# Token tiles 4 to 15 of the projections: normalised rows pass through DRAM and are turned by 32x32 blocks on VectorE

## What is computed

```
x  = L0_attn_x                                  # (2, 1024, 1024) float32
xn = (x - mean(x)) / sqrt(var(x) + 1e-5)        # over the last axis
q, k, v = xn @ wq, xn @ wk, xn @ wv             # 1024 -> 32, 8, 8 heads of 32
q, k = rope(q), rope(k)                         # pairs of neighbours rotated
s = softmax(q @ k.T / sqrt(32) + causal) @ v    # four query heads to one key head
s = s @ wo
w_gu, w_d = 4-bit weights times scales
h = silu(xn @ w_gu[:, :2752]) * (xn @ w_gu[:, 2752:])
out = x + s * silu(h @ w_d)
```

## Time and profile before

| | |
|---|---|
| median of 3 runs | 2204.02 us |
| time of the profiled execution | 2204.33 us |
| its span, first to last instruction | 2202.6 us |
| TensorE busy | 99% of the span |
| VectorE, GpSimd, ScalarE busy | 69%, 61%, 46% |
| granted TensorE clock, mean | 0.999 |

### The profile page before, as it was taken

One profiled execution on the slowest core, in us unless ns is written; L12 is line 12 of the kernel. 1 busy time (PEld: TensorE's weight loads), 2 busy tenths in 40 slices (PEclk: granted clock), 3 DMA queues, 4 the chain that ended last, 5 costly groups with the idle time before them and its releaser, 6 DMA issues.

```text
span 2202.6 us, 39253 instructions
## 1 busy us (share of the span) xinstructions
PE 2179.7 (99%) x14856; PEld 1106.4 (50%) x14856; DVE 1523.5 (69%) x2272; ACT 1014.1 (46%) x1918; POOL 1334.6 (61%) x1398
## 2 busy tenths in 40 slices
PE   7999999999999999999999999999999999999998
PEld 4555545555555555555555555444444444444443
DVE  5677767777777777777777773377858865555564
ACT  4333156666666666666666667344322221111211
POOL 4855588788878887888878888367620013332332
PEclk9999999999999999999999999999999999999999
DMA  6344212433243332333333333455359874333332
GB/s 206 99 109 101 48 33 59 74 64 59 63 76 76 68 51 71 71 73 69 59 66 66 74 52 61 72 164 172 101 163 327 277 262 149 110 110 110 110 116 89
DMA packets 296128, 230.01 MB, mean 104 GB/s; under 512 B 191664, under 2 KB 260782, under 8 KB 292868
## 3 DMA queue, kind: packets, MB, share of 16 engines
q1 hardware_dynamic: 295940, 227.51, 39.9%
HBM read 136.54 MB, written 90.78 MB: 103 GB/s over the span
## 4 chain that ended last, share of the span: by engine, by line
PE 97%; DVE 1%; ACT 1%; issue 1%; POOL 0%; DMA 0%; DVEq 0%; ACTq 0%; POOLq 0%
PE gu_ps L1183 39%; PE out_ps L1897 9%; PE qk_ps L726 9%; PE out_ps L1877 8%; PE mx_ps L1080 6%; PE sc_ps L1124 6%; PE dn_ps L1886 5%; PE dn_ps L1897 4%; PE o_ps L1146 4%; PE v_ps L709 2%; PE o_ps L1150 2%; PE sz_ps L1093 2%; PE sz_ps L1098 1%; PE tr_ps L695 1%; PE dn_ps L1889 1%
## 5 line engine op out<-in xcount | busy, mean ns | idle before, releaser
L1183 PE MATMUL gu_ps<-xT,wg 128*128 128x512 f16 x4128 | 983.7, 378 | 0.4 <-DVE h L1454 0.4
L1518 POOL TENSOR_TENSOR room<-room 128x1152 f16<-128x1152 f32 x256 | 539.2, 2106 | 40.7 <-ACT room L1232 27.8
L1183 PEld LDWEIGHTS gu_ps<-xT,wg 128*128 128x128 f16 x4128 | 367.7, 97 | 377.6 <-DVE h L1454 0.9
L1232 ACT ACTIVATE room<-sc_ps 128x512 f32<-128x512 f32 (+3 forms) x768 | 349.0, 489 | 369.1 <-PE sc_ps L1124 365.4
L2244 POOL TENSOR_TENSOR xT<-arena,xT 128x1024 f16<-128x1024 f32 x40 | 85.1, 2129 | 411.1 <-ACT xT L2012 411.1
L1513 POOL TENSOR_SCALAR_AFFINE_SELECT room<-room 128x128 f32<-128x128 f32 x512 | 143.8, 296 | 140.8 <-ACT room L1232 140.8
L1361 DVE TENSOR_REDUCE part<-mx_ps 128x2 f16<-128x1024 f32 x128 | 157.0, 1227 | 100.3 <-PE mx_ps L1080 100.2
L1361 DVE TENSOR_REDUCE shift<-mx_ps 128x2 f16<-128x1024 f32 (+3 forms) x256 | 212.8, 831 | 8.8
L726 PE MATMUL qk_ps<-xT,w 128*128 128x512 f16 x960 | 212.8, 379 | 0.0
L1124 PE MATMUL sc_ps<-arena 97*128 97x512 f16 (+3 forms) x768 | 209.7, 327 | 2.3 <-ACT room L1232 2.1
L1146 PE MATMUL o_ps<-arena,room 128*128 128x65 f16 x2240 | 191.1, 191 | 0.0
(11 more groups left out here) (181 smaller groups left out, 3203.1 us busy)
## 6 DMA issues: line engine op xcount, KB each, us to landing
hidden_scratch<-hT SPq DMA_DIRECT2D x84, 256.0 KB, 3.0
o_scratch<-room SPq DMA_DIRECT2D x64, 260.0 KB, 9.7
room<-o_scratch SPq DMA_DIRECT2D x16, 1040.0 KB, 7.7
hT_in<-hidden_scratch SPq DMA_DIRECT2D x11, 1344.0 KB, 7.5
arena<-q_scratch SPq DMA_DIRECT2D x48, 256.0 KB, 3.8
stock<-in_qw_d SPq DMA_DIRECT2D x42, 256.0 KB
down_scratch<-wd SPq DMA_DIRECT2D x84, 128.0 KB, 2.8
xin<-in_x SPq DMA_DIRECT2D x16, 512.0 KB, 4.6
```

Source lines behind the costliest of these rows:

```text
L1183: last = pe.matmul(to[:, :], wg[:, u, wp, s, cols], xT[:, xp, s, tokens], start=(s == 0 and k == 0), stop=(s == KT - 1 and k == 2))
L1232: act.activation(probs[:, r % 2, START[t] + c:START[t] + e], sc_ps[n % SC_BANKS][:, 0:e - c], ACT.Exp, scale=float(1.0 / np.sqrt(HD))).the ...
L1518: pool.tensor_tensor(p_lo[:, r % 2, c], probs[:, r % 2, c], p_hi[:, r % 2, c], ALU.subtract).then_inc(lo_done, 1)
```

## The change

Tiles 0 to 3 are handled as before. For tiles 4 to 15 the halves are no longer formed and turned on TensorE. The float32 rows `xn` are stored to a DRAM scratch tensor and loaded back by four transfers, each to 32 partitions, so that 32 tokens lie on 32 partitions four times over. VectorE turns the 32x32 blocks with four instructions into one float32 tile `x32`; ScalarE copies `x32` to the high half of `xT`, and GpSimd subtracts that from `x32` into the low half. The schedule tables are new, `SPLIT_AT` and `LOAD_AT` are added. `x32` is also the buffer into which x tile 2 is loaded. `xh` and `xl` share their memory with the two buffers `xt`. In the later stages a wait of VectorE for its own reciprocal goes, and two semaphores become one.

```diff
-        xin = sb("xin", [P, XB, D], F32)
+        two_in = sb("xin", [P, 2, D], F32)
         xn = sb("xn", [P, 2, D], F32)
-        xh = sb("xh", [P, 2, D], F16)
-        xl = sb("xl", [P, 2, D], F16)
+        xt = sb("xt", [P, 2, D], F32)
+        x32 = sb("x32", [P, D], F32)
+        xin = [two_in[:, 0, :], two_in[:, 1, :], x32[:, :]]
...
-        NORM_AT = {0: 0, 2: 1, 4: 2, 5: 3}
-        TURN_AT = {3: 0, 5: 1, 7: 2, 8: 3}
+        NORM_AT = {0: 0, 1: 1, 3: 2, 5: 3}
+        LOAD_AT = {1: 0, 2: 1, 4: 2, 6: 3}
+        TURN_AT = {3: 0, 5: 1, 6: 2, 8: 3}
+        SPLIT_AT = {4: 0, 6: 1, 7: 2, 9: 3}
...
             def load_x(n):
-                if n >= XB:
-                    sp.wait_ge(xn_done, n - XB + 1)
+                if n >= 3:
+                    sp.wait_ge(xn_done, {3: 2, 4: 1}.get(n, n - 1))
...
+            def store_normed(n):
+                sp.wait_ge(xn_done, n + 1)
+                sp.dma_start(xn_d[n], xn[:, n % 2, :]).then_inc(xn_stored[n % 2], 16)
+
+            def load_turned(n):
+                if n < CHT + 2:
+                    sp.wait_ge(xh_turned, CHT)
+                    sp.wait_ge(xl_turned, CHT)
+                else:
+                    sp.wait_ge(xt_turned, n - CHT - 1)
+                sp.wait_ge(xn_stored[n % 2], 16 * ((n - CHT) // 2 + 1))
+                for k in range(P // 32):
+                    sp.dma_start(xt[32 * k:32 * (k + 1), n % 2, :].rearrange("j (t c) -> j t c", c=D // 4),
+                                 xn_d[n, :, k * (D // 4):(k + 1) * (D // 4)].rearrange("(t j) c -> j t c", j=32)
+                                 ).then_inc(xt_loaded[n % 2], 16)
...
-            load_x(6)
             for e in range(NCH * CT):
                 tc, j = e // CT, e % CT
+                if tc + 1 < NCH and j in NORM_AT:
+                    store_normed((tc + 1) * CHT + NORM_AT[j])
+                if tc + 1 < NCH and j in LOAD_AT:
+                    load_turned((tc + 1) * CHT + LOAD_AT[j])
                 load_tables(e)
...
# gpsimd, at the end of a step
+            def low_turned(n):
+                tokens = slice(n * P, (n + 1) * P)
+                pool.wait_ge(xTh_done, n + 1)
+                pool.wait_ge(xTl_done, n)
+                pool.tensor_tensor(xT[:, 1, :, tokens], x32[:, :].rearrange("p (s t) -> p s t", s=KT),
+                                   xT[:, 0, :, tokens], ALU.subtract).then_inc(xTl_done, 1)
...
-                if j in NORM_AT and tc + 1 < NCH:
-                    low_x((tc + 1) * CHT + NORM_AT[j])
+                if j in SPLIT_AT and tc + 1 < NCH:
+                    low_turned((tc + 1) * CHT + SPLIT_AT[j])
...
# scalar
+            def high_turned(n):
+                act.wait_ge(xt_turned, n - CHT + 1)
+                act.activation(xT[:, 0, :, n * P:(n + 1) * P], x32[:, :].rearrange("p (s t) -> p s t", s=KT), ACT.Copy
+                               ).then_inc(xTh_done, 1)
...
-                if tc + 1 < NCH and j in TURN_AT:
-                    turned((tc + 1) * CHT + TURN_AT[j])
+                if tc + 1 < NCH and j in SPLIT_AT:
+                    high_turned((tc + 1) * CHT + SPLIT_AT[j])
...
                     spread((tc + 1) * CHT + NORM_AT[j])
-                    high_x((tc + 1) * CHT + NORM_AT[j])
...
# vector
+            def turn(n):
+                dve.wait_ge(xt_loaded[n % 2], 64 * ((n - CHT) // 2 + 1))
+                if n == CHT:
+                    dve.wait_ge(xn_done, 3)
+                else:
+                    dve.wait_ge(xTh_done, n)
+                    dve.wait_ge(xTl_done, n)
+                for k in range(P // 32):
+                    cols = slice(k * (D // 4), (k + 1) * (D // 4))
+                    last = dve.transpose(x32[:, :].rearrange("p (s t) -> p s t", s=KT)[:, :, 32 * k:32 * (k + 1)],
+                                         xt[:, n % 2, cols].rearrange("p (i s) -> p s i", s=KT))
+                last.then_inc(xt_turned, 1)
...
                 tables_at(e)
+                if tc + 1 < NCH and j in TURN_AT:
+                    turn((tc + 1) * CHT + TURN_AT[j])
                 if tc + 1 < NCH and j in NORM_AT:
                     norm((tc + 1) * CHT + NORM_AT[j])
...
# tensor
                 queries_keys(e)
-                if j in TURN_AT and tc + 1 < NCH:
-                    turn((tc + 1) * CHT + TURN_AT[j])
...
# third stage, vector
-            dve.reciprocal(rsum[:, u, :], parts(u)[:, :, HD]).then_inc(rsum_done, 1)
+            dve.reciprocal(rsum[:, u, :], parts(u)[:, :, HD])
...
-            dve.wait_ge(rsum_done, n + 1)
```

More of the change, by code:

```diff
@@ L179, in project_qkv @@
                 g_idx_d, qwg, zw, scw, szt, rest, mid, qwd, idx, gu_loaded, dn_loaded, idx_loaded, table_step,
-                qw_loaded, z_d):
+                qw_loaded, z_d, xn_d):
     bn, mv, std, rstd, eps = small
@@ L210, in project_qkv @@
         sb("fill", [P, room_words - (KT * QKV + 2 * S + 6 * BANK + KV * VW)], F32)
-        xin = sb("xin", [P, XB, D], F32)
+        two_in = sb("xin", [P, 2, D], F32)
         xn = sb("xn", [P, 2, D], F32)
-        xh = sb("xh", [P, 2, D], F16)
-        xl = sb("xl", [P, 2, D], F16)
+        xt = sb("xt", [P, 2, D], F32)
+        x32 = sb("x32", [P, D], F32)
+        xin = [two_in[:, 0, :], two_in[:, 1, :], x32[:, :]]
+        xh = xt[:, 0, :].bitcast(F16).rearrange("p (u c) -> p u c", u=2)
+        xl = xt[:, 1, :].bitcast(F16).rearrange("p (u c) -> p u c", u=2)
         qk_ps = [bank(f"qk_ps{i}", [P, BANK], F32) for i in range(2)]
@@ L241, in project_qkv @@
         xTl_done = sem("xTl_done")
+        xn_stored = [sem(f"xn_stored{i}") for i in range(2)]
+        xt_loaded = [sem(f"xt_loaded{i}") for i in range(2)]
+        xt_turned = sem("xt_turned")
         qk_ready = sem("qk_ready")
@@ L285, in project_qkv, with x_place, x_count @@
         x_v = x.rearrange("b (t p) d -> (b t) p d", p=P)
-        NORM_AT = {0: 0, 2: 1, 4: 2, 5: 3}
-        TURN_AT = {3: 0, 5: 1, 7: 2, 8: 3}
+        NORM_AT = {0: 0, 1: 1, 3: 2, 5: 3}
+        LOAD_AT = {1: 0, 2: 1, 4: 2, 6: 3}
+        TURN_AT = {3: 0, 5: 1, 6: 2, 8: 3}
+        SPLIT_AT = {4: 0, 6: 1, 7: 2, 9: 3}
+        def x_place(n):
+            return 2 if n == 2 else n % 2
+        def x_count(n):
+            return 16 * (n // 2 if n >= 4 and n % 2 == 0 else (n + 1) // 2 if n % 2 else 1)
         def block_of(j):
@@ L313, in load_x @@
             def load_x(n):
-                if n >= XB:
-                    sp.wait_ge(xn_done, n - XB + 1)
-                sp.dma_start(xin[:, n % XB, :], x_v[n]).then_inc(x_loaded[n % XB], 16)
+                if n >= 3:
+                    sp.wait_ge(xn_done, {3: 2, 4: 1}.get(n, n - 1))
+                sp.dma_start(xin[x_place(n)], x_v[n]).then_inc(x_loaded[x_place(n)], 16)
+            def store_normed(n):
[12 more added lines that the diff above has]
+                                 ).then_inc(xt_loaded[n % 2], 16)
             def load_w(i):
@@ L388, in sync @@
                 if j % 2 == 1 and j // 2 < CHT:
-                    n = tc * CHT + j // 2 + 3 + CHT
+                    n = tc * CHT + j // 2 + 2 + CHT
                     if n < TT:
@@ L544, in norm @@
                 u = n % 2
-                dve.wait_ge(x_loaded[n % XB], 16 * (n // XB + 1))
+                own = xin[x_place(n)]
+                dve.wait_ge(x_loaded[x_place(n)], x_count(n))
                 for h in range(2):
-                    last = dve.bn_stats(bn[:, h, :], xin[:, n % XB, h * BANK:(h + 1) * BANK])
+                    last = dve.bn_stats(bn[:, h, :], own[:, h * BANK:(h + 1) * BANK])
                 last.then_inc(bn_done, 1)
@@ L553, in norm @@
                 dve.wait_ge(rstd_done, n + 1)
-                if n >= 2:
+                if 2 <= n < CHT + 2:
                     dve.wait_ge(xl_done, n - 1)
-                dve.tensor_scalar(xn[:, u, :], xin[:, n % XB, :], mv[:, u, 0:1], rstd[:, u, :],
+                if n >= CHT + 2:
+                    dve.wait_ge(xn_stored[u], 16 * ((n - CHT) // 2))
+                dve.tensor_scalar(xn[:, u, :], own, mv[:, u, 0:1], rstd[:, u, :],
                                   ALU.subtract, ALU.mult).then_inc(xn_done, 1)
+            def turn(n):
[10 more added lines that the diff above has]
+                last.then_inc(xt_turned, 1)
             def low_w(i):
@@ L668, in vector @@
                 if e == (NCH - 1) * CT:
-                    dve.wait_ge(xh_done, TT)
-                    dve.wait_ge(xl_done, TT)
+                    dve.wait_ge(xTh_done, TT)
+                    dve.wait_ge(xTl_done, TT)
                 if tc == NCH - 1:
@@ L1617, in finish @@
         FREED = {B_M6: [(0, 1)], B_M7: [(1, 1)], B_M4: [(1, 0), (0, 0)]}
-        rsum_done = sem("rsum_done")
         joined = sem("joined")
@@ L1637, in finish @@
         wk_loaded = sem("wk_loaded")
-        tail_loaded = sem("tail_loaded")
         block_loaded = [sem(f"block_loaded{i}") for i in range(SUMS + 2)]
@@ L1829, in sync @@
```

(8 more changed lines are left out.)

## The result

The changed kernel takes 2241.11 us (median, 2240.53 to 2242.05) against 2204.01 us for the one before; the ratio is 1.0169, with a 95% interval of 1.0151 to 1.0186. It is 37.1 us slower, where I forecast 16 slower and a range up to 2236. The direction was right, the size was not.

What follows compares the result with a forecast made beforehand. TensorE, busy 99% of the time, was taken to bound the kernel. The terms -11.8 + 12.4 + 6.4 + 4.2 + 4.6 = +15.8 us on 2204.3 gave 2220 us, with a range from 2207 to 2236.

Steps and rivals of the forecast that it cites:

- the 11.8 us: TensorE's transpositions of 12 tiles at 0.98 us, all on the path, forecast as won by removing them.
- The direct chain: Each chunk's end: last query and key result through VectorE, ScalarE, GpSimd to the fourth split; wait at least 4.2 us.
- The clock: Slower TensorE clock after gaps: 2.3 us for each of the two longer, nothing for the third, 4.6 us.
- 12.4, 6.4 and 4.2 us: Forecast waits of TensorE at the ends of chunks 0, 1 and 2.
- 1.3 us a tile, which I take: VectorE's four transpositions of a tile, at 0.31 us each from the pace of the 32-lane swap.
- the upper bound of 2.6: VectorE's transpositions of a tile at the pace of the table comparison, 2.6 us for 1024 columns.
- in all 21.6: Chunk 1: us from VectorE's start of step 16 through the three last splits, chained by transpositions.
- so 2.9 us late: Chunk 1: VectorE's lateness from step 15; TensorE's step 16 result leads the values' end by 18.1 us.
- tables of 0.7 us there; it is on time: Chunk 2: short table work, so no late start, and the direct chain's 4.2 us decides.
- Chunk 0: VectorE and GpSimd followed step by step: TensorE waits from 87.1 to 99.5, 12.4 us.
- Slow transpositions: Rival: 2.6 us a tile, 1.3 more, eight in series, 10.4 us more, 2230; chance 18%.
- The late queue: Rival: reloads late, a queue held up by new waits puts each chunk's end some 4 us later, 2232; 8%.

Runs made afterwards that it cites:

- e2: The changed kernel with GpSimd's low half of a turned tile at the start of its step, not the end: 2225.86 us, ratio 1.01.
- e6: The changed kernel with SyncE's load of x and store of the values both ahead of the step's table loads: 2237.62 us, ratio 1.0153.
- e9: As e8, with SyncE's queue reordered (x loads first, table transfers in step 17, heads' loads in steps 25 and 27): 2198.47 us, ratio 0.9978.
- e3: The changed kernel with only SyncE's load of x moved ahead of the step's table loads: 2240.02 us, ratio 1.0165.
- e4: The changed kernel with one of a tile's four transpositions, three quarters of the turned data left out: 2230.72 us, ratio 1.0119.
- e10: As e7, with the same order of SyncE's queue as e9: 2206.96 us, ratio 1.0012.
- e8: As e7, but tiles 4 to 7 turned on TensorE with the old schedule, only tiles 8 to 15 through DRAM: 2209.81 us, ratio 1.0027.
- e7: The changed kernel with the orders of e2 and e6, transpositions ahead of table parts, and a schedule one to two steps earlier: 2218.17 us, ratio 1.0061.

## Why the prediction was right and wrong

**Right:** what bounds the kernel; the 11.8 us; that they would be eaten by a wait of TensorE for GpSimd's low half of the fourth tile at three chunk ends; that the reload lands in time (3.1 and 4.1 us, and no transposition waits for it). The direct chain has the length that I gave it, 6.6 us from the last swap to the end of the split (176.01 to 182.57; 154.89 to 161.5 in the prediction), but it decided no gap: VectorE began it 13.5 us after TensorE's result of 162.46. The clock was put at 4.6 us, 2.3 for each of two gaps and nothing for the third, and measured at 4.4, as 1.4, 1.7 and 1.3. That the sums agree is luck: in e2 to e6 the same three pieces lost 5.9 to 6.7 us.

**Wrong, the sizes of the gaps:** 12.4, 6.4 and 4.2 us were forecast, 23.0 in sum; 14.46, 17.47 and 11.78 came, 43.7. The 20.7 us between them are the whole error. The steps that failed:

1. *VectorE's transpositions, "1.3 us a tile, which I take".* They last 606 ns and follow each other at 0.53 us, 2.13 us a tile. The pace of the swap was the wrong neighbour; the upper bound of 2.6 was nearer. The Trainium skill (VectorE: DVE Perf Modes, "The three transpose paths") has 311 ns for half the elements and a quarter of the bytes per partition; 606 ns agrees with its double, while the tile's 2.13 us goes by the shorter distance of 0.53. The same page's "Rules for kernel authors" names TensorE for a 128x128 transposition whose result may go to PSUM; the whole change, 37.1 us slower, agrees, and e9, in which VectorE turns eight tiles and 5.6 us are won, does not. The term is 0.8 us a tile, so 1.7 us in the chain of chunk 1 and as much in that of chunk 2.
2. *The chain of chunk 1, "in all 21.6".* It was 27.5, in chunk 2 too. Two transpositions account for 1.7 of the 5.9 us between them. 2.9 more are VectorE's own work in step 18: the fourth tile's transposition could have begun when the third split ended, at 168.86 + 2.12 = 170.98, but began at 173.90, behind the sum and a table part (3.0 in chunk 2). I had walked the chain from split to transposition as if VectorE had nothing between. The rest, 1.3, is 0.4 in each of the two ways from swap to split, 6.6 and not 6.2, and 0.5 in the first link.
3. *The start of chunk 1's chain, "so 2.9 us late".* It was 155.12 - 146.9 = 8.2 us late. I looked at SyncE's queue for what the change adds and not for what already stood in it, 9.7 us of table transfers ahead of a load of x that the change issues one tile later. e3 and e6 show both waits that come of it. In e6, without them, it is 3.0 us late. That meets my 2.9 through two errors that cancel: the table part took 1.49 + 1.52 us and not 2.35 + 1.64, and the transposition took 2.2 and not 1.3.
4. *Chunk 2, "tables of 0.7 us there; it is on time".* The 0.7 us are the table part of another step. That of step 25, which corresponds to step 15, was 3.4 us long in the kernel before (its rows stand below this list). In the changed kernel it takes 2.4 us, the transposition follows and then `norm`, and VectorE reaches step 26 at 230.94, when TensorE's result has been there since 223.35 + 5.18 = 228.5: 2.4 us late. So the long chain decides there and not the direct one of 4.2.
5. *Chunk 0* was followed step by step and came within 2.1 us. Two and a half transpositions at 0.8 us are enough for that, and e4 took 4.0 us from this gap, two and a half at 1.6; that it is these alone is worked out, not tried.

VectorE's table part of step 25 in the kernel before:

```profile
197.60 2.11 DVE L158 CAST stock<-stock 8x256 bf16<-8x256 f32 x1
199.73 1.24 DVE L159 CAST stock<-stock 32x256 bf16<-32x256 f32 x1
```

With these the sums close: 27.5 + 8.2 - 18.1 = 17.6 for the 17.47 of chunk 1, and 27.5 + 2.4 - 18.1 = 11.8 for the 11.78 of chunk 2. Of the 20.7 us the transpositions are 5.5, VectorE's work ahead of the fourth one 5.9, the late starts 7.7 (5.3 in chunk 1, of which e6 shows 5.2 to be the queue, and 2.4 in chunk 2), and the rest small terms.

No rival had it. Slow transpositions was true in its mechanism, but at 0.8 us in place of 1.3 its eight in series make 6.6 us and not 10.4. The late queue, priced at 4 us a chunk and given 8%, was a queue behind table transfers that had stood there before, holding a load of x and a store and not a reload, in chunk 1 alone. VectorE's own table parts, ahead of the fourth tile's transposition and in step 25, stood in no rival, and that several causes could hold at once was not in my chances.

## What to carry to other kernels

Work moved off the bound engine pays only if what replaces it is finished before the bound engine asks for it; write down the full chain at each hand-over, with everything that each engine has in its order between two links, tables and memsets included. Look at the issuing queue as at an engine: here two batches of 14 transfers took 9.7 and 7.6 us, in which no load or store behind them started. Where one stretch can't hide the new work, apply the change only to the stretches that can: with the same orders and the same queue e9 wins 0.22% and e10, the change in all three chunks, loses 0.12%; with the orders first chosen it lost 1.7%.

## What the runs showed of the hardware

What a gap costs in clock did not follow its length. In the profiles of the changed kernel and of e2 to e8, each of the twenty gaps of 5.4 us and more was followed by a piece that took 1.3 to 2.9 us too long; the dearest was the 5.84 us of e8, and the 17.47 us of the changed kernel cost 1.7. Shorter ones went both ways: 1.98 us in e8 cost 1.7, 3.38 in e10 cost 1.4 and 3.49 in e7 cost 2.7, but 1.88 and 2.05 in e7 and 3.76 in e10 cost nothing. The Trainium skill (TensorE: Matmul & The Clock Gate, "Why this matters for your kernels") warns of idle gaps between bursts of matmuls; the traces agree for the long ones. The two rows of e8:

```profile
155.13 12.21 PE L802 MATMUL qk_ps<-xT,w 128*128 128x512 f16 x48 [1.98 <-POOL xT L461]
...
225.10 8.26 PE L802 MATMUL qk_ps<-xT,w 128*128 128x512 f16 x24 [5.84 <-POOL xT L461]
```

e9 is less steady than the kernel before: its eleven runs lie between 2197.33 and 2202.15 us, the kernel before beside it between 2203.8 and 2204.91. The mean granted clock goes with it, 1.0 in the two fastest runs of e9 (2197.33 and 2197.63) and 0.998 in the two slowest (2202.02 and 2202.15). That these had a short gap which the profiled run lacks would fit, but only the fastest run has a profile, so it is not shown.
